# A graph network layer on one core: sort steps dealt over fewer tiles, work started at its own half tiles, row gathers that read their indices in place

## What is computed

```python
N, D, R, E = 1250, 1024, 8, 20000           # nodes, width, relations, edges
# layer 0: relational graph convolution with a gate
out = x @ root + bias
for r in range(R):
    mask = (edge_type == r)
    sums = segment_sum(x[src] * mask, dst); cnt = segment_sum(mask, dst)
    out = out + (sums / max(cnt, 1)) @ weight[r]
z = concat([out, x]) @ w_gate + b_gate
x = layernorm(x + tanh(out) * z + x * (1 - z))
# layer 1: graph convolution with self loops and symmetric norm
deg = segment_sum(1, dst); dinv = rsqrt(deg)
x = layernorm(x + relu(segment_sum((x @ W)[src] * dinv[src] * dinv[dst], dst) + b))
```

## Time and profile before

| | us |
|---|---|
| median of 3 runs | 1794.18 (1793.83 to 1794.49) |
| the profiled execution's own time | 1797.81 |
| its span | 1796.0 |
| PE busy (matmul) | 1669.5 |
| DVE busy | 1052.9 |
| POOL busy | 888.6 |
| ACT busy | 565.9 |

### The profile page before, as it was taken

The page is one execution under the profiler, slowest core; times in us unless marked ns, Lnnn a source line. Parts: engine busy times, 40 slices in busy tenths (PEclk is TensorE's granted clock), DMA queues, the critical chain, the costliest instruction groups (busy, mean ns, idle before and its releaser), DMA issues.

```text
span 1796.0 us, 22772 instructions
## 1 busy us (share of the span) xinstructions
PE 1669.5 (93%) x7621; PEld 1352.8 (75%) x7621; DVE 1052.9 (59%) x1937; ACT 565.9 (32%) x923; POOL 888.6 (49%) x879
## 2 busy tenths in 40 slices
PE   7999999905999999999999999999999879999997
PEld 6888888704777777888888888878878667777786
DVE  4446300005665766477777762878688885555486
ACT  3221111201333333354544542545455431111000
POOL 0008777776777772366656531767577421121000
PEclk9999999957999999999999999999999889999999
DMA  6313333220122122567666634676666642443643
GB/s 222 112 48 95 96 96 96 50 54 27 39 86 83 45 86 89 205 204 226 179 216 206 185 109 169 199 231 201 194 210 201 224 153 91 153 152 111 260 154 106
DMA packets 115115, 254.30 MB, mean 142 GB/s; under 512 B 25061, under 2 KB 25436, under 8 KB 114870
## 3 DMA queue, kind: packets, MB, share of 16 engines
q0 software_dynamic: 39904, 89.23, 18.1%
q1 hardware_dynamic: 41142, 92.41, 15.1%
q10 hardware_dynamic: 33952, 71.20, 10.6%
HBM read 185.13 MB, written 77.80 MB: 146 GB/s over the span
## 4 chain that ended last, share of the span: by engine, by line
PE 67%; DVE 7%; issue 2%; POOL 1%; another core or an unknown queue 0%; ACT 0%; DMA 0%; DVEq 0%; ACTq 0%; POOLq 0%
PE PG L694 42%; PE PM L718 9%; PE PG L783 6%; PE PG L852 5%; PE PM L705 3%; PE PG L802 2%; DVE X L1336 1%; DVE STATS L1330 1%; DVE XLO L1071 1%; DVE X L1353 1%; DVE GATE L1352 1%; PE PM L791 1%; PE PM L772 0%; DVE TANH L1342 0%
## 5 line engine op out<-in xcount | busy, mean ns | idle before, releaser
L694 PE MATMUL PG<-WHI,XHI 128*128 128x512 f32 x1600 | 637.4, 398 | 70.1 <-DVE WLO L1071 70.1
L694 PE MATMUL PG<-WHI,XLO 128*128 128x512 f32 x1600 | 627.1, 392 | 0.0
L694 PE MATMUL PG<-WLO,XHI 128*128 128x512 f32 x1600 | 626.9, 392 | 0.0
L694 PEld LDWEIGHTS PG<-WHI,XHI 128*128 128x128 f32 x1600 | 302.5, 189 | 134.9 <-DVE WLO L1071 68.6
L694 PEld LDWEIGHTS PG<-WHI,XLO 128*128 128x128 f32 x1600 | 302.1, 189 | 63.9
L694 PEld LDWEIGHTS PG<-WLO,XHI 128*128 128x128 f32 x1600 | 302.2, 189 | 60.8
L1071 DVE TENSOR_TENSOR WLO<-WRAW,WHI 128x512 fp32r<-128x512 f32 x176 | 124.5, 718 | 225.9 <-ACT WHI L875 214.7
L611 POOL DMA_INDIRECT WORK<-y,IDX x176 | 191.8, 1090 | 121.2 <-DVE SPLO L1226 55.4
L882 ACT ACTIVATE STAGE<-PG 128x512 f32<-128x512 f32 x200 | 118.9, 594 | 410.0 <-PE PG L694 401.6
L611 POOL DMA_INDIRECT RAW<-y,IDX x176 | 192.7, 1095 | 86.5 <-DVE SPLO L1226 44.2
L536 POOL DMA_INDIRECT records<-RREC,IDX x160 | 204.6, 1279 | 61.0 <-issue 43.7
(11 more groups left out here) (168 smaller groups left out, 1897.6 us busy)
## 6 DMA issues: line engine op xcount, KB each, us to landing
y<-STAGE ACTq DMA_DIRECT2D x200, 256.0 KB
WRAW<-in_L_gnn_weight_dram SPq DMA_DIRECT2D x30, 1024.0 KB
WRAW<-in_L_gnn_w_gate_dram SPq DMA_DIRECT2D x8, 1024.0 KB
WORK<-y SPq DMA_DIRECT2D x10, 512.0 KB, 6.3
GATE<-y SPq DMA_DIRECT2D x10, 512.0 KB
x<-X ACTq DMA_DIRECT2D x10, 512.0 KB, 6.0
WORK<-x SPq DMA_DIRECT2D x10, 512.0 KB, 4.7
WORK<-in_x_dram SPq DMA_DIRECT2D x9, 512.0 KB, 3.7
```

What stands on the lines that cost most here:

```text
L694: last = pe.matmul(PG[:, bank, :], lhs[:, k, t * P:(t + 1) * P], rhs[:, j % 2, k, :], start=(k == 0 and n == 0), stop=(k == KT - 1 and n = ...
```

## The change

Five edits, all in when and where work is issued; every matmul, every split and every gather of data stays.

1. The sort pieces are dealt over tiles 0 to 11: two scans at some tiles, PE's sums after tile 7 (`OFFSETS_JT = 7`, it was 14), group starts and first positions at tile 8, the rest at tile 9, `pair_groups` at tile 11.
2. `count_setup` stands before step 128 instead of 112.
3. Count pairs stand at steps 133 to 212 (88 pairs over 80 steps, 8 steps with two) instead of 120 to 207; run 0 at 226 to 310 (85 steps, 3 with two) instead of 220 to 307; run 1 at 325 to 399 without the break (75 steps, 13 with two).
4. POOL's row gathers take their indices from `REC[:, tile, 0:1]`. The copies to `IDX` (22 a run) and their waits are gone, and so is POOL's first wait for the weights.
5. A few small buffers change places (`IDENT` behind `WGOT`), and DVE waits once for `dinv_ready` before run 0.

```diff
+OFFSETS_JT = NT - 3
-COUNT_AT = (3, 0)
-RUN0_AT = (5, 20)
-RUN1_BODY = 8
-SETUP_AT = (2, 32)
-LATE = 5
-DENSE = NPAIR // 2
+SETUP_STEP = 128
+COUNT_FROM, COUNT_TO = 133, 213
+RUN0_FROM, RUN0_TO = 226, 311
+RUN1_FROM, RUN1_TO = 325, 400
+
+def spread(start, end):
+    steps = end - start
+    bounds = [k * NPAIR // steps for k in range(steps + 1)]
+    return {start + k: range(bounds[k], bounds[k + 1]) for k in range(steps)}
...
-                def gather_half(i, b, peeled, run=run):
-                    if not (peeled and run == 0):
-                        after(pool, msg_split, i * (2 * RING) + (run * ETILES + b * RING - RING))
-                    pool.wait_ge(sorted_in, 16)
-                    nc.gpsimd.tensor_copy(IDX[:, b, :], REC[:, bass.ds(i * (2 * RING) + b * RING, RING), 0]).then_inc(idx_set, 1)
-                    pool.wait_ge(idx_set, i * 2 + (IDX_BASE2 + run * 2 * turns_w + b + 1))
-                    for j in range(RING):
...
+                for tile in range(ETILES):
+                    after(pool, msg_split, tile + run * ETILES - (ROWS - 1))
+                    pool.sem_inc(passed_pool, 1)
+                    pool.indirect_dma_start(
+                        out=raw[tile % ROWS], out_offset=None, in_=y_d[0:(run + 1) * YROWS, :],
+                        in_offset=bass.IndirectOffsetOnAxis(ap=REC[:, tile, 0:1], axis=0),
+                        bounds_check=(run + 1) * YROWS - 1, oob_is_err=False).then_inc(got[tile % ROWS], 16)
...
-                if jt == 14:
+                if jt == OFFSETS_JT:
+                    pe.wait_ge(x_split, 2 * (OFFSETS_JT + 2))
                     pe.wait_ge(rows_total, 1)
...
-            nothing = steps(None, None)
-            plain((2, 0), SETUP_AT, nothing)
+            steps(2 * SUBSTEPS, SETUP_STEP)
             count_setup()
-            plain(SETUP_AT, COUNT_AT, nothing)
-            one_each(dve, COUNT_AT, steps(count_hot, count_add), count_add)
+            steps(SETUP_STEP, COUNT_TO, COUNT_PAIRS, count_hot, count_add)
             dve.wait_ge(count_out, 16)
```

More of the change, by code:

```diff
@@ L57 @@
 AHEAD = 2
-COUNT_AT = (3, 0)
-RUN0_AT = (5, 20)
-RUN1_BODY = 8
-SETUP_AT = (2, 32)
-LATE = 5
-DENSE = NPAIR // 2
[L70 to L119, removed]
+SETUP_STEP = 128
+COUNT_FROM, COUNT_TO = 133, 213
+RUN0_FROM, RUN0_TO = 226, 311
+RUN1_FROM, RUN1_TO = 325, 400
+STEPS_ALL = SUBSTEPS * (UNITS_Y + 4) // 2
+def spread(start, end):
+    steps = end - start
+    bounds = [k * NPAIR // steps for k in range(steps + 1)]
+    return {start + k: range(bounds[k], bounds[k + 1]) for k in range(steps)}
+COUNT_PAIRS = spread(COUNT_FROM, COUNT_TO)
+RUN0_PAIRS = spread(RUN0_FROM, RUN0_TO)
+RUN1_PAIRS = spread(RUN1_FROM, RUN1_TO)
 class Chain:
@@ L720, in message_pair, with steps @@
                 last.then_inc(pair_done, 1)
-            def steps(pair_step):
-                def step(i, s, pairs):
-                    i, s = normal(i, s)
-                    gemm(i, s // 2, s % 2)
-                    for pair, n in pairs:
-                        pair_step(pair, n)
-                return step
+            def steps(start, end, pairs={}, pair_step=None):
+                for s in range(start, end):
+                    gemm(s // SUBSTEPS, s % SUBSTEPS // 2, s % 2)
+                    for pair in pairs.get(s, ()):
+                        pair_step(pair, pair)
             pe.sem_inc(cells_done, AHEAD)
@@ L914, in take_counts, with steps @@
                                      PM[:, 2 * (n % 2):2 * (n % 2) + 2, 0:NCOL // 2], ACT.Copy).then_inc(cells_taken, 1)
-            def steps(run, counts=False):
-                def step(i, s, pairs):
-                    i, s = normal(i, s)
+            def steps(start, end, pairs={}, run=None):
+                for s in range(start, end):
                     if run is not None:
-                        for pair, n in pairs:
-                            msg_high(pair, n, run)
+                        for pair in pairs.get(s, ()):
+                            msg_high(pair, pair, run)
                     if s % 2 == 0:
-                        i, jt = (i, s // 2 - 1) if s > 0 else (i - 1, TILES_BODY - 1)
+                        i, jt = (s // 2 - 1) // TILES_BODY, (s // 2 - 1) % TILES_BODY
                         evac(i, jt)
@@ L927, in step @@
                         store_y(i, jt)
-                    if counts:
-                        for pair, n in pairs:
-                            take_counts(pair, n)
-                return step
+                    if run is None:
+                        for pair in pairs.get(s, ()):
+                            take_counts(pair, pair)
             act.sem_inc(cells_taken, AHEAD)
@@ L1234, in msg_add, with steps @@
                 dve.wait_ge(pair_added, pair + (run * NPAIR + 1 + AHEAD))
-            def steps(prepare, add):
-                def step(i, s, pairs):
-                    i, s = normal(i, s)
-                    for pair, n in pairs:
-                        prepare(pair, n)
-                        if n > 0:
-                            add(pair - 1, n - 1)
-                    if s % 2 == 0 and s > 0:
-                        w_low_next(i, s // 2 - 1)
-                return step
+            def steps(start, end, pairs={}, prepare=None, add=None):
+                for s in range(start, end):
+                    for pair in pairs.get(s, ()):
+                        prepare(pair, pair)
+                        if pair > 0:
+                            add(pair - 1, pair - 1)
+                        if pair == NPAIR - 1:
+                            add(pair, pair)
+                    if s % 2 == 0 and s % SUBSTEPS > 0:
+                        w_low_next(s // SUBSTEPS, s % SUBSTEPS // 2 - 1)
             dve.sem_inc(pair_added, AHEAD)
```

88 lines of the change are left out of this document (35 added, 53 removed).

## The result

| | before | changed |
|---|---|---|
| median, us | 1794.12 (1793.83 to 1794.49) | 1720.68 (1720.01 to 1724.05) |
| ratio to before | 1 | 0.9594 (0.9578 to 0.9611) |
| profiled execution, us | 1797.81 | 1724.05 |
| its span, us | 1796.0 | 1722.3 |

The changed kernel is 73.4 us faster; forecast were 69.3 and 1725. In the pages alone the span lost 73.7.

A forecast was written before the change was run, and what follows sets the result against it. PE, busy 1669.5 of 1796.0 us, was taken as the bound, with only its waits and slow-clock stretches to win. Terms -67.8 + 1 + 6.0 - 8.5 = -69.3 off 1794.18 gave 1725 us, range 1716 to 1737.

The forecast's parts named there:

- run 0: First run of message pairs and row gathers: PE lost nothing there, so the missing copies stay hidden; 0 us.
- The gap at step 120: PE's wait at step 120 goes: 65.9 us and 1.8 of slow restart, together -67.8.
- The records: Sorted records reach DVE at 367.7, before the setup at about 376.5; 14 us of cover before the first count pair.
- records late: Rival: chunks stop POOL's scatter twice as long, records come at 387, 5 us past the cover; 1730 us, chance 0.04.
- The wait behind the counts: At unit 11, PE waits 4.2 us for slices behind the counts' write and clearing; with slow clock +6.0.
- The clock behind that wait: Behind the 4.2 us wait at unit 11, PE's matmuls restart at the lower clock; +1.8 us.
- Run 1: POOL lacks slack in run 1; without copies and evenly spread, 3 of 11.6 us loss stay: -8.5, between 0 and -11.6.
- The rival of slow transfers: Late rows in run 1 come from slow transfers; 8.5 lost, 1733 us; chance 0.15 for keeping at least half the loss.
- Gathers in place: Row gathers reading indices in place cost what those from IDX cost, mean 1.095 us.
- The rivals that had them dearer: Row gathers dearer in place: 1741 us at 1.7 a row, 1869 at 2.1; chances 0.05 still faster, 0.02 slower.
- The counts: Eight doubled steps within the counts cost +1 us, an estimate between 0 and 4.
- The terms that were off: Forecast: until step 133 0, counts +1, wait behind them +6.0, run 0 0, run 1 -8.5, behind last message pair 0.

The follow-up runs named there:

- e1: Kernel before with only the sort pieces dealt over tiles 0 to 11; setup, counts, gathers and run 1 as before; 1753.42 us, ratio 0.9805.
- e2: Changed kernel with the sort pieces back at tiles 0 to 18 as before; 1751.32 us, ratio 0.9788 to the kernel before.
- e7: Changed kernel with the counts' second pairs one step earlier, so step 212 has one pair; 1769.77 us, ratio 0.986, on a widely scattering chip.
- f1: Changed kernel itself once more, on a quieter chip; 1725.97 us, ratio 0.9618 to the kernel before.
- f4: Changed kernel with the counts at steps 133 to 210; 1722.78 us, ratio 0.9602 to the kernel before.
- e8: Changed kernel with counts at steps 133 to 207 and run 1's second pair of step 399 moved to 398; 1746.46 us, ratio 0.97, widely scattering chip.
- e3: Changed kernel with run 1 in two dense stretches as before, indices still read in place; 1722.55 us, ratio 0.9629 to the kernel before.
- e4: Changed kernel, run 1 evenly spread, with the copies to IDX and their waits back; 1722.92 us, ratio 0.9634 to the kernel before.
- e5: Changed kernel itself again, on a chip where every kernel scattered widely; 1779.68 us (1750.35 to 1786.48).

## Why the prediction was right, point by point

- **The gap at step 120** was the sum's main term and came as worked out. e1 and e2 show that it hangs both on the records' time and on where the setup and the counts stand.
- **The records** came at 372.8, not 367.7: positions 1.2 us later than I said, the scatter 277.3 instead of 276.1, and the load issued 4.45 after the last scatter rather than about 2. So the cover at the setup was 4 us, where my times gave 9, and ahead of the first count pair some 10 instead of 14. The rival "records late" didn't come, but it was closer than its 0.04 says. The half turn of 12.82 that I took as quiet lay in DVE's idle 77.97 us, so it says nothing of weight slices; others before, which had them, took 12.82 to 13.41. The Trainium skill, "SBUF — State Buffer", section "Who interferes with whom", has a DVE instruction with two SBUF inputs contend with a GpSimd instruction that reads SBUF. In the changed kernel's scatter 34 scatters had slices and nothing else of DVE beside them; against 1.18 us each they took 2.7 us more in all (23 and 1.1 before), so the cost is small here. For the split beside POOL's add, above, the traces have 2.1 us.
- **The wait behind the counts** had the right mechanism and place, and was mis-sized: 8.2, not 6.0. I took DVE and POOL from the last pair's end T to the write as T + 2.0, as in the earlier trace rows. But step 212 has two pairs, their adds wait for one another (665.85 and 667.45), and the write starts at 668.58, T + 3.0 with T = 665.54. That, and 0.6 in the rest of the way, put unit 11 at T + 24.8 instead of T + 23.2, and PE's wait at 5.9 instead of 4.2. e7 confirms it from the other side: with one pair the write starts at T + 2.0 again (672.21 and 674.21). I had counted the cost of doubled pairs within the counts and not at their end.
- **The clock behind that wait**: I charged 1.8, the trace has 2.3 (f1 1.4). The Trainium skill, "TensorE: Matmul & The Clock Gate", section on HAM oscillation, has waiting gaps behind which the work starts cold; this trace agrees for the 5.7 us. Behind 0.95 us in f4 and 1.27 ahead of run 1's last pair no slow matmul follows. Between these, length alone didn't decide: behind 2.51 us in e7 the granted clock is 0.58 (1084.1 to 1088.0), behind 2.47 in e8 it is 1.00 (1083.5 to 1087.0). My reason, that 4.2 lies above the 2.03 of the earlier trace rows, was thinner than I thought.
- **Run 1** lost 1.5, and I had left 3. The reason, POOL without slack, is borne out by e3, e4 and POOL's waits, and one of its numbers was off: 1.095 is the mean gather of both runs. In run 1 alone the means were 1.163 (`RAW`) and 1.102 (`WORK`), so a row cost 1.58 us where 1.54 was asked; in the changed kernel they are 1.098 and 1.086. The rival of slow transfers is out as a cause by itself, since all five kernels of the table move the same rows; what a slow one adds where POOL has no slack wasn't measured. The size is luck in part: some 2.5 of the 10.2 is the place at 1203.9, and against e1 the change took 6.1. The 1.59 before the last pair I put down to the two pairs of the last step; the traces show POOL's add beside the split.
- **Gathers in place** cost no more: 1059 and 1075 ns against 1095 and 1090 in the earlier trace rows and its sister group. The rivals that had them dearer didn't come.
- **The counts** are the term with the wrong sign, +1 against -2.5. That is ACT's standstill in the profiled execution of before: against e1 (290.4, less eight steps 268.6) the changed kernel's 268.8 leave 0.2 for the doubled steps. I had taken "a few us in the counts" for a property of the kernel.

The terms that were off (+0.7, -3.5, +2.2, -0.7, -1.7, -1.4) sum to -4.4, so part of the closeness is luck of signs, within a range of 21 us that they didn't strain.

## What to carry to other kernels

A wait on a queue that also feeds the bounding engine costs what is queued behind it: move the waiting work behind those feeds, and check its new neighbours at both ends, since the same queue had a wait (the write of the counts) that twelve steps used to hide and seven didn't. When work is dealt over steps by rounding, look at what the last step holds: two pairs there cost 1.4 us of PE, where eight doubled steps within the counts cost 0.2 in a quiet execution. Where a producer only just keeps its consumer's pace, any slack ends the loss, so count remedies once; and take the producer's pace from the stretch in question, not from a mean over the whole kernel. And a loss that one trace shows may belong to that execution: 2.5 us of the counts and 2.5 of run 1 did.

## What was unexpected in the hardware

- ACT stood still for up to 12 us at a time in the counts in some executions, in the same code, 79.5 us in e5 and none in e1 to e4. Of the 69 such waits in the nine traces that have them, 42 come behind the issue of a store of `y` and 27 behind another copy of counts. All lie where POOL issues its small gathers of 1/count, but that stretch covers nearly all of the counts. The cause stayed open; no experiment separated anything here.
- The number of slow matmuls behind nearly equal waits differs: ten behind 5.7 us in the changed kernel's trace, six behind 5.78 in f1.
- A DVE split that started beside or behind POOL's add took 2.86 to 2.93 us, and 0.75 where it started 0.02 or 0.06 us ahead of it.
- The granted clock of the changed kernel's profiled execution is below that of other executions with no longer spacing of its matmuls: in a stretch at full pace (500 to 600) the record has 0.95, f1's has 1.00, and both have 0.227 a matmul. Clock by core, the changed kernel and then f1, the same program:

```profile
core 0: 1722.3 us, clock 0.939
```

```profile
core 0: 1722.2 us, clock 0.989
```

The spans agree within 0.1 us, so that column, at this level, is no measure of time here.
